# Another written-out order for five engines in a two-layer transformer kernel, with three exponential buffers and two masked ones

## The reference

```python
x = x + _L0_attn_a_ref(_layernorm(x), W_qkv, b_qkv, W_out, b_out)
x = x + _L0_ffn_ref(_layernorm(x), w_gate, w_up, w_down)
x = x + _L0_attn_b_ref(_layernorm(x), w_qkv, b_qkv, w_proj, b_proj)
x = x + _L0_ffn_ref(_layernorm(x), w_gate, w_up, w_down)
# attention: softmax of q k^T / sqrt(32) under a causal mask, times v, then the output projection
# ffn: (silu(x w_gate^T) * (x w_up^T)) w_down^T
```

## Time and profile before

| | before |
|---|---|
| median of 3 runs | 1995.39 us (1995.38 to 1996.1) |
| the profiled execution | 1995.06 us, span 1993.3 us |
| granted PE clock over the span | 0.999 |
| PE busy | 1957.7 us (98%) |
| DVE, ACT, POOL busy | 1188.4 (60%), 803.7 (40%), 983.5 us (49%) |

### The profile page before, as it was taken

The page is one execution under the profiler, slowest core; times in us unless marked ns, Lnnn a source line. Parts: engine busy times, 40 slices in busy tenths (PEclk is TensorE's granted clock), DMA queues, the critical chain, the costliest instruction groups (busy, mean ns, idle before and its releaser), DMA issues.

```text
span 1993.3 us, 27851 instructions
## 1 busy us (share of the span) xinstructions
PE 1957.7 (98%) x10288; PEld 1438.2 (72%) x10288; DVE 1188.4 (60%) x2387; ACT 803.7 (40%) x1478; POOL 983.5 (49%) x767
## 2 busy tenths in 40 slices
PE   6999999999999999999999999999999999999999
PEld 5655588888765558888875656888887565688887
DVE  4777465445578845544567884545456777554544
ACT  2388532221248752222115874222211687332221
POOL 4025369763212537975421252897532225289740
PEclk9999999999999999999999999999999999999999
DMA  5334011121333301311252340111113234012111
GB/s 139 90 86 111 3 55 62 54 64 32 72 82 93 97 21 44 106 45 62 74 138 65 86 97 23 42 64 54 53 32 96 65 86 97 12 53 64 53 43 42
DMA packets 58821, 132.37 MB, mean 66 GB/s; under 512 B 10560, under 2 KB 11584, under 8 KB 58688
## 3 DMA queue, kind: packets, MB, share of 16 engines
q1 hardware_dynamic: 58688, 130.60, 24.3%
HBM read 75.51 MB, written 4.19 MB: 40 GB/s over the span
## 4 chain that ended last, share of the span: by engine, by line
PE 87%; DVE 6%; issue 4%; ACT 2%; POOL 1%; DMA 1%; SPq 0%; DVEq 0%; POOLq 0%; ACTq 0%
PE bank L1488 11%; PE bank L1354 10%; PE bank L1356 10%; PE bank L1355 10%; PE ring L1354 9%; PE ring L1356 9%; PE ring L1355 9%; PE bank L1461 8%; PE ring L1430 8%; PE ring L1345 1%; DVE xn L1051 1%; ACT kq_parts L844 1%; DVE stats L1014 0%; POOL area L657 0%; DVE xt_lo L1060 0%
## 5 line engine op out<-in xcount | busy, mean ns | idle before, releaser
L732 POOL TENSOR_SCALAR_AFFINE_SELECT prob<-prob 128x512 f32<-128x512 f32 x128 | 83.7, 654 | 509.5 <-ACT prob L861 379.2
L861 ACT ACTIVATE prob<-bank 128x512 f32<-128x512 f32 (+1 forms) x512 | 271.8, 572 | 135.0 <-PE bank L1461 125.2
L1168 DVE TENSOR_TENSOR x<-x,bank 128x512 f32<-128x512 f32 x256 | 170.5, 685 | 232.3 <-PE bank L1356 231.7
L657 POOL TENSOR_TENSOR area<-w_stage,area 128x1024 fp32r<-128x1024 f32 x126 | 302.1, 2398 | 10.5
L655 POOL TENSOR_SCALAR area<-w_stage 128x1024 fp32r<-128x1024 f32 x126 | 144.3, 1145 | 301.1 <-PE bank L1356 189.7
L1098 DVE CUSTOM_DVE_ANT_0 xn<-ring,mask_row 128x384 bf16<-128x384 f32 (+7 forms) x384 | 244.9, 661 | 70.1 <-PE ring L1430 65.7
L1354 PE MATMUL ring<-xt_hi,area 128*128 128x512 f32 x672 | 263.9, 393 | 1.3 <-DVE area L1201 1.3
L1356 PE MATMUL ring<-xt_hi,area 128*128 128x512 f32 x672 | 262.1, 390 | 0.0
L1355 PE MATMUL ring<-xt_lo,area 128*128 128x512 f32 x672 | 262.1, 390 | 0.0
L1461 PE MATMUL bank<-area 98*128 98x512 f32 (+3 forms) x768 | 233.2, 372 | 2.3 <-DMA area<-nm_lo 1.4
L1430 PE MATMUL ring<-area 96*128 96x512 f32 (+3 forms) x768 | 221.7, 360 | 2.9 <-DVE row_max L1098 2.1
(11 more groups left out here) (171 smaller groups left out, 3643.9 us busy)
## 6 DMA issues: line engine op xcount, KB each, us to landing
w_stage<-ffn_w SPq DMA_DIRECT2D x96, 512.0 KB, 3.5
area<-kq_parts SPq DMA_DIRECT2D x336, 128.0 KB, 2.4
w_stage<-attn_w SPq DMA_DIRECT2D x32, 512.0 KB, 4.8
area<-attn SPq DMA_DIRECT2D x48, 128.0 KB, 3.3
x<-x_in SPq DMA_DIRECT2D x16, 256.0 KB, 3.9
out<-x SPq DMA_DIRECT2D x16, 256.0 KB, 2.0
bias_rows<-row_bias SPq DMA_DIRECT2D x8, 256.0 KB, 4.2
masked<-x_in SPq DMA_DIRECT2D x6, 256.0 KB, 4.5
```

The costliest lines, as they stand in the source:

```text
L657: pool.tensor_tensor(lo, src, hi.bitcast(F32), ALU.subtract).then_inc(w_split, 1)
L861: act.activation(prob[:, step % PROB_BUFS, h, off:], scores_at(u, j, h), ACT.Exp, scale=SCALE).then_inc(prob_ready, 1)
L1168: dve.tensor_tensor(x[:, t, :], x[:, t, :], row_bank(s, n)[:, :], ALU.add).then_inc(rows_drained, 1)
```

## The change

The five order strings are replaced. `HEAD_OF_RING` gets v of tiles 0 and 1 first, ahead of q and k of unit 0. `PROB_BUFS` goes from 2 to 3, `MASKED_BUFS` from 3 to 2. No engine gets or loses work: the letters of each kind are as many as before (464 on PE).

```diff
-HEAD_OF_RING = (("q", 0), ("k", 0), ("v", 0), ("v", 1), ("ln1", 2), ("ln1", 3), ("q", 1), ("k", 1))
+HEAD_OF_RING = (("v", 0), ("v", 1), ("q", 0), ("k", 0), ("ln1", 2), ("ln1", 3), ("q", 1), ("k", 1))
...
-PROB_BUFS = 2
+PROB_BUFS = 3
...
 ORDER = (
-    "pppppfffffffpfpppppfffffpppffpfpfpffpfpfpffpfpfpfpffpffpffpf",
+    "ffffffppffpppppffffppfpffpfpfpfpfpfppfpffppfpfpffppfpffpffpffpf",
...
 POOL_ORDER = (
-    "dbbwmmmbmmwmmbmmmmmwmmmbwmmmmmwbaaawammmambmmmbamammdmmwdw",
+    "bbdwbwwmmmbbmwbmbmmmmmmmmmmmmmmmawaawammammmmwmmabamdmmmwd",
...
-MASKED_BUFS = 3
+MASKED_BUFS = 2
```

More of the change, by code:

```diff
@@ L202 @@
 ORDER = (
-    "pppppfffffffpfpppppfffffpppffpfpfpffpfpfpffpfpfpfpffpffpffpf",
[L204 to L211, removed]
+    "ffffffppffpppppffffppfpffpfpfpfpfpfppfpffppfpfpffppfpffpffpffpf",
+    "ssfsfssfsfsvfsfvsfsssfvfsssfvvffpsffpff",
+    "svsfsfpfsfspfsfsvfssvfsfsvsfsfsfsfvssffsvsffssvvvsffssvsfsssfvvsssfsfvvvf",
+    "ssfsfsffssfvsfssfsfvspspfsfsvffssvffpff",
+    "ssfpssffvsfsfvsffsffsfsfsfsfvfsfvfsfvsfsfssfsfsfsffssvsssffssssvssfvff",
+    "ssvvfsspsppssvvfsfpsssffsvsfssfsvf",
+    "ssffvsffsfsfsvffssffvsfsfvsfsfssfssfsvsffssvsfsfsvsssffssssvss",
+    "sfsfsvsfsvsfsfsvvfssssfssssv",
+    "ssvvvssfssvssvssvssffssvssvssfssfssvvvvvssfssssfssssvvvv",
 )
@@ L215 @@
     "xxxxxxx",
[L216 to L223, removed]
+    "eexeeeeeeeeee",
+    "eoeexeeeexeeeeeeeereeerereerereerreereerr",
+    "eeorxeerxeeerrerreeexe",
+    "eexeeeeeeoeereerrerrereeereerexerxeeeerereerr",
+    "eereeroereeexeeexe",
+    "eeeeeeoeeeeeeeeeeeeeeeeeeeeee",
+    "eeeeeoeeeeeee",
+    "eeoeeeeeeeeeeeeeeeeeeeeeeeeexeox",
 )
 DVE_ORDER = (
-    "mnnnnmnmnnmmmqmqmmqmmmmqmmmmmmmmqmqmmmmmmmqmmmqmmmmmmmmmmmmmmmmmmqmmrmqmmmmmmmmmmrmrmmrmmmmmrrrmrmmmmrmr"
-    "hmrmrrrmmrmrmmmmqmmqmrmmmmmrmrmmrrmmmrmmmrmrmmmmmmmmmhmmmmmmmmmqrmmrqrmrmmrmmrmmrmmmmmmmrmmmmmmmmmmrrrrr"
+    "nmnnmnnnmnmmmqmmmqmmmmmqmmmmmmmqmmqqmmmmmqmmmmmqmmmmmmmmmmmmmmmmrmqmrmmrqmmrmmmmrmmmmmmmrrmmmmrmrrmrrrmm"
+    "mmmhmmrrmmmmqmmmrmqmmmmmmmmmmmmmrmmmrrrmrmmmmmmrrmmrmhmmmmqmmmqmmmmmmmmrmmrmrmmmrmmrrmmrmmrmmmmmmmmrrrrr"
     "rrrmmmmnnnrrrrrrrrlmm",
@@ L234 @@
 POOL_ORDER = (
-    "dbbwmmmbmmwmmbmmmmmwmmmbwmmmmmwbaaawammmambmmmbamammdmmwdw",
+    "bbdwbwwmmmbbmwbmbmmmmmmmmmmmmmmmawaawammammmmwmmabamdmmmwd",
 )
 SP_ORDER = (
-    "klkkklkklkkmkkkkmkkmkkkklkmkkkklmkklkkkmkkklmlkml",
+    "lkkklkklkkkmkkkmkllkkmkkkkkkmklkkkmkkkkmkkkmklmll",
 )
```

## The result

| | before | changed |
|---|---|---|
| median of 5 executions | 1995.39 us (1994.24 to 1996.1) | 1982.96 us (1981.08 to 1984.82) |
| profiled execution | 1995.06 us, span 1993.3 | 1981.08 us, span 1979.4 |
| ratio | | 0.9938 [0.9924, 0.9953] |

The change makes the kernel 12.4 us faster. The forecast was 17.8 us: the time lies inside the range of 1965 to 1988, 5.5 us above the point. It lies outside the 1972 to 1981 that the prediction gave to its own forecast, and almost where the rival "only the fixed places pay" had put it (1983.3).

What follows compares the result with a forecast made beforehand. PE, busy for 98% of the span, was taken as the bound. Eight terms for gaps summed to -17.8 us; from the profiled 1995.1 us, with 0.3 added for the median, this gave 1977.5 us, range 1965 to 1988.

Steps and rivals of the forecast that it cites:

- only the fixed places pay: Rival: only the first product and the two pairs of transposes bring time, 12.1 us, giving 1983.3; chance 0.22.
- first product of a stage: Start of attention stages: v of tile 0 needs only pair 0 of "ln1", so PE starts earlier; 3.5 us faster.
- transposes of "ln1" pair 2: Head of the attention stage: PE's 1.20 us wait for the pair's normalisation goes in four iterations; 4.8 us faster.
- transposes of "ln2" pair 2: At "ln2": PE's 0.96 us wait for the ring, held by the first hidden tile, goes; 3.8 us faster.
- fewer runs of small products: Attention stages: 50 runs instead of 55, each costing 0.30 us more than its products; 6.0 us faster.
- ring use behind unit 1's multiplication: Unit 1: no POOL split or bias addition meets DVE's multiplication, so PE's wait behind it goes; 2.2 us faster.
- scores behind exponentials: Score matmuls that follow closely on the exponentials freeing their banks wait more; 3 us slower.
- two masked buffers: Units 3 and 5: DVE's maxima wait for ACT to leave a masked buffer; 1.5 us slower.
- three exponential buffers: ACT waits less for products to free a buffer; 2 us faster.
- More than the sum: Rival: third buffer and spread row sums also cut waits on exponentials, 8 to 10 us more, about 1968; chance 0.16.
- nothing: Rival: a gap closed at one place opens at the next, within 4 us of 1995.4; chance 0.07.
- slower: Rival: maxima wait for ACT with two masked buffers and PE stands; in full 29 us slower, 2024; chance 0.08.

Runs made afterwards that it cites:

- the old middle: The old order with head and tail changed, given three exponential buffers and three masked buffers in bf16: 1980.37 us.
- The first experiment: The kernel before with only the head of the attention stage (PE, POOL, DVE) and the end of POOL's string changed: 1980.55 us.
- the second: The kernel before with only the last two letters of POOL's order exchanged: 1991.6 us.
- the inverse deviation's experiment: The first experiment's kernel with POOL making the inverse deviation ahead of its bias additions again: 1983.98 us.
- Both experiments that moved products: Changed kernel, five products moved behind the next ring step: 1995.12 us. Old order with head, tail and two splits moved, one product of unit 0 moved up: 1987.92 us.
- The lighter ACT: The changed kernel with ACT's 32 row sum exponentials an iteration cut to 128 columns: 1980.77 us.
- the first experiment's kernel with the lighter ACT: The first experiment's kernel with ACT's row sum exponentials cut to 128 columns: 1980.56 us.
- the kernel of the further merged product: The old order with head, tail and two weight splits moved, and one product of unit 0 moved up to the run before it: 1987.92 us.

## Why the prediction was right, and what it missed

For the terms I counted, in each profiled execution, from PE's starts what every step of the four attention stages takes beyond the undisturbed distance of a step of its kind. The measured column compares the kernel before with the changed one, in us over four iterations.

| term | forecast | measured |
|---|---|---|
| first product of a stage | -3.5 | -3.7 |
| transposes of "ln1" pair 2 | -4.8 | -5.8 |
| transposes of "ln2" pair 2 | -3.8 | -4.7 |
| fewer runs of small products | -6.0 | -6.8 |
| ring use behind unit 1's multiplication | -2.2 | -2.2 |
| scores behind exponentials | +3.0 | +1.7 |
| two masked buffers | +1.5 | 0 |
| three exponential buffers | -2.0 | 0 |
| other uses of the ring | none | +3.7 |
| products that wait | none | +2.0 |
| side projections and the end of the stage | none | +1.1 |
| TensorE's lower clock in the first iteration | none | +0.5 (2.2, before 1.7) |

The sum is -14.2, the spans differ by 13.9. The zeros of the two buffer terms are from the experiments, that of the exponential buffers from the old middle. (The last step of the prediction's sum, 1977.3 and 0.3, gives 1977.6 and not 1977.5.) How the rest divides depends on what is called undisturbed: with the lowest tenth of each pair of kinds, and a step behind a run of products as a kind of its own, the runs give -5.2, the scores +2.5, the other uses of the ring +2.4 and the products +1.9.

*First product, "ln1", "ln2": right in mechanism, and somewhat larger than forecast.* In the first iteration PE starts at 16.67 us and not at 17.98, in the others the gap is gone. The first experiment gives these three together as 14.8 us by the medians, the second "ln2" alone, the inverse deviation's experiment the part of POOL's order at "ln1". As the prediction said, pair 3 is late next: it is what waits as soon as the collision is back.

*Fewer runs: the price was right, and it was paid back.* 0.32 us a run by experiment against 0.30 read from the earlier trace rows; by my count the undisturbed time of a stage fell from 216.2 to 214.5 us. The step that failed is the one behind it. The prediction saw only one way in which a merged product could cost, that it waits for its own exponentials, and one way in which scores could lose. It left out what a product does where it stands: it is the work that PE does while DVE takes a maximum. Both experiments that moved products show this in rows, 0.84 us at unit 1's transpose and 1.03 at the third of three uses of the ring, and in the changed kernel the uses of the ring other than unit 1's cost 3.7 us more and the products 2.0. One of those in the changed kernel, unit 5's first maxima, which the new order has among unit 3's products:

```profile
629.82 0.82 DVE L1093 CUSTOM_DVE_ANT_0 masked<-ring,mask_row 128x640 f32<-128x640 f32 x1
...
630.25 0.19 PEld L1461 LDWEIGHTS bank<-area 98*128 98x128 f32 x1 [0.33 <-ACT prob L861]
630.71 0.30 PEld L1430 LDWEIGHTS ring<-area 96*128 96x128 f32 x2 [0.27 <-DVE row_max L1093]
```

A maximum is in hand until 630.57, and PE has one score between. That products cover the ring is shown at the two experiments' places; that each of the many small waits of the new middle comes from it is argued, and for two groups of them it is not so. The longest wait of a ring use in the changed kernel, 0.73 us at 139.69, is for the DMA that stacks k; the change rewrites the order of these DMAs too, and the prediction has no term for it. And of the 2.0 us of the products, 1.6 are one product of unit 5, which comes 0.40 us late in each iteration:

```profile
688.37 0.69 DVE L1136 TENSOR_TENSOR attn<-attn,recip 128x512 f32<-128x512 f32 x1
...
688.52 1.04 POOL L732 TENSOR_SCALAR_AFFINE_SELECT prob<-prob 128x512 f32<-128x512 f32 x1 [2.91 <-ACT prob L861]
...
689.70 0.85 PE L1488 MATMUL bank<-prob,v 128*32 128x384 f32 x8 [0.27 <-POOL prob L732]
```

DVE's multiplication starts 0.15 us before the mask, the mask takes 1.04 us where one alone takes 0.63, and PE waits for it. All the kernels with the new middle have this wait, and none with the old one. So a collision of the kind that the change removed is made anew by it, the other way round: DVE holds up POOL. The prediction looked for a late mask in unit 6; it is in unit 5.

*Scores behind exponentials: the sign was right, the size some half to four fifths.* Such a place in the changed kernel, second iteration:

```profile
555.40 0.69 ACT L844 ACTIVATE kq_parts<-bank,bias_qk 128x512 fp32r<-128x512 f32 x1
...
555.87 0.40 PE L1461 MATMUL bank<-area 98*128 98x512 f32 x1
...
556.63 0.19 PEld L1461 LDWEIGHTS bank<-area 98*128 98x128 f32 x1 [0.80 <-ACT prob L861]
```

The next score comes 0.76 us after this one, where a score's own spacing is 0.23, because ACT has a projection to take before the exponential that frees the bank. It recurs in all four iterations. The lighter ACT changes nothing there (0.73 us): what counts at this place is what stands just ahead of an exponential, not how busy ACT is.

*Two masked buffers: the mechanism was right, and the changed order escapes it.* 21.7 us in the old order, inside the 0 to 48 that the bounds allowed; nothing that could be measured in the new.

*Three exponential buffers: mis-sized.* ACT's waits for products, 13.8 us in the earlier trace rows, reach PE nowhere in the old middle. For the new middle it is not shown.

*The collision: right.* The ring use behind unit 1's multiplication waited 2.2 us over the four iterations and waits no more. By the rule of the SBUF page of the Trainium skill (SBUF — State Buffer, "two separate sides") the prediction had made the term lower, at 1.5, for masks that may hold the lock. No multiplication in the changed kernel takes over 0.694 us, but no mask began ahead of one there: where they meet, in unit 5, the multiplication began first, and the mask was held up. In the kernel with two masked buffers in the old order a mask is first, and the multiplication takes 1.05 us:

```profile
660.35 0.64 POOL L733 TENSOR_SCALAR_AFFINE_SELECT prob<-prob 128x512 f32<-128x512 f32 x1
...
660.48 1.05 DVE L1137 TENSOR_TENSOR attn<-attn,recip 128x512 f32<-128x512 f32 x1
```

So masks do hold up a multiplication, and the term came out whole because none was in front.

The rivals: "only the fixed places pay" has the size (1983.3), and the first experiment shows it as a mechanism: the middle gives nothing. It isn't that nothing happens there: by the table 9.0 us are won (runs and collision) and 7.4 lost (scores, ring, products). That the measured time comes so near to 1983.3 is in part luck: the fixed places gave 14.2 us where 12.1 were counted, and what the rest lost made up for it. "More than the sum" and "nothing" are refuted, "slower" too, though its price stands in the old order.

## What to carry to other kernels

Where a written-out order is changed, price the places that are plain in the trace (a collision beside a wait, a product in front of its data) and try them alone: here they gave all of the gain, and with one more collision removed 5 us more than the new order of everything. Before a filler is moved or merged, ask which wait it covers where it stands: its own saving was 0.3 us, its cover 0.8 to 1.0. A buffer count is worth nothing or 22 us depending on the order around it, so it is to be tested in the order in which it will run. Where a POOL instruction is moved towards a DVE one, look at both for the wait: here one collision went and another came.

## What the runs showed of the hardware

*A mask of POOL and an operation of DVE hold each other up.* A mask alone takes 0.63 us, a multiplication 0.69. Whichever began second was the longer one: the mask 1.04 us at 688.52, the multiplication 1.05 at 660.48.

*TensorE's clock falls for a few us behind some stops.* In the first iteration of the kernel before and of the changed one, PE works after a stop of 2.48 us and of 0.78 us, and for a while the matmuls lie 0.43 us apart instead of 0.23. The timeline of the changed kernel:

```profile
16.67 0.77 PE L1354 MATMUL ring<-area,xt_hi 128*128 128x512 f32 x1 [0.78 <-DVE xt_lo L1060]
...
17.66 0.63 PE L1356 MATMUL ring<-area,xt_lo 128*128 128x512 f32 x1
18.08 0.63 PE L1354 MATMUL ring<-area,xt_hi 128*128 128x512 f32 x1
...
21.57 0.39 PE L1354 MATMUL ring<-area,xt_hi 128*128 128x512 f32 x1
```

Ten such steps cost 2.0 us. In the kernel before, the windows show the lower of the two levels (1.2 GHz) over them, with the granted clock third from the end:

```profile
19.00:20.00 1.00, 1.00 (x4) 0.79 (x3) 0.00 (x0) 0.00 (x0) 0.94 (x1) 0.50 0.00 0
20.00:21.00 1.00, 1.00 (x4) 0.81 (x3) 0.00 (x0) 0.00 (x0) 0.92 (x2) 0.50 0.00 0
```

In the changed kernel the windows read 1.00 over the same spacing. Its trace has no record of the clock before 21.14 us, and the view puts 1.00 where there is none, so that only the spacing tells the level there. The profiled execution of the first experiment, with the same products in this place, doesn't have them at all. In the kernel with two masked buffers in the old order the lower level appears in the middle of the work. Its windows:

```profile
1652.00:1653.00 1.00, 0.93 (x10) 0.46 (x10) 0.50 (x1) 1.00 (x3) 0.92 (x2) 0.86 0.00 0
1653.00:1654.00 1.00, 1.00 (x10) 0.51 (x3) 1.00 (x3) 0.61 (x3) 1.00 (x1) 0.50 0.00 0
...
1656.00:1657.00 1.00, 1.00 (x5) 0.76 (x5) 0.42 (x1) 0.00 (x0) 0.00 (x0) 0.93 0.00 0
```

PE had stood for 1.10 us, and the granted clock is at half behind it, until 1656. In the first experiment's kernel with the lighter ACT the same is seen behind a stop of 1.59 us for a DMA, at 621.61: 0.50 in 623 to 625. But the kernel of the further merged product had a stop of 1.67 us, at 132.47, with the granted clock at 1.00 behind it. The two kernels with stops of a us in each stage (this one and the further merged product) have the lowest mean clocks over their executions, down to 0.995 and 0.996, while all five executions of the first experiment have 1.000 and lie within 1.2 us. The changed kernel's range from 0.998 to 1.000, and 0.002 of 1980 us would be most of the 3.7 us between them. So a wait of a us may cost its own length and, in some executions, part of the clock behind it. That the stops are the cause is not shown, and what decides in which executions is open.
